# Routing and final residual of a slot-routing layer: one scaling moved to ScalarE, the last adds shared by two engines

## The chip, the cores and the metric

The kernel runs on one Trainium2 chip, on all 8 of its cores, each with its own batch element and its own copy of the weights. The cores do not talk to each other. The metric is the device time in microseconds (us) of the slowest core; the median over runs is given. Each core has TensorE (matmuls, output in PSUM), VectorE, ScalarE, GpSimd (here the adds that work on SBUF) and SyncE, which here only issues DMAs.

## The reference

Per batch element, `x` is 4096 tokens by 1024 channels in float32.

```python
x = x + _layernorm(_L0_attn_ref(_layernorm(x)))     # causal mean over the tokens
x = x + _layernorm(_L0_ffn_ref(_layernorm(x), ...)) # the part below
# inside _L0_ffn_ref, NUM_SLOTS = 64, TOP_K = 8
h = gelu(ctx @ w1 + b1)                             # ctx = [x, mean slot]
route_logits = (h @ w2 + b2) / (abs(tau) + 0.1)
alpha = softmax over the top 8 of 64 slots, zero elsewhere
slot_input = einsum('bts,btd->bsd', alpha, x)       # gathered into slots
# a GRU step, attention among the slots, a layernorm, a projection
slot_values = y @ wvp + bvp
out = einsum('bts,bsd->btd', alpha, slot_values)    # back to the tokens
return out @ wo + bo
```

## The kernel before

The 4096 tokens are 32 tiles of 128 (`NT = 32`), and the whole of `x` stays in SBUF as `sb_x` from the first load to the last store. The program is a row of stages, and in each every engine has its own instruction list; the order is written out by hand, with explicit semaphore waits. Helpers record the semaphore value after each ScalarE instruction (`SACT`, L207) and VectorE instruction (`VTS` L178, `VTT` L173, `VBN` L192 and so on), so that other engines can wait for it by name, as `V(("fn", j), 0)`.

1. First residual: layernorm of each tile (`x1b`), causal sums with triangular matmuls into two PSUM tiles (`pcs`), a second layernorm (`anb`, two halves), and GpSimd adds `anb` to `sb_x` (L412).
2. Router: layernorm (`x3b` on ScalarE), transpose, matmuls with `w1`, gelu, matmul with `w2`; the logits end up in `sb_L`.
3. Routing, L600 to L651, for each tile `j`: VectorE finds the 8 largest logits (`VMX`, MAX8) and a bias (`eb`), ScalarE takes the exp (`sb_E`), VectorE masks and sums it (`aub`), takes the reciprocal and writes `sb_alpha`, and then scales the tile of `sb_x` by the layernorm's scale to bf16 in `x2bf`, two halves in turn. TensorE multiplies `sb_alpha` with `x2bf` into `p_si` and transposes `sb_alpha` into `p_at`, and every fourth tile VectorE copies four transposed tiles to `sb_alphaT`, for which it waits for TensorE.
4. Slots: SyncE loads `Wih` transposed into `whhT` once TensorE has finished all routing tiles; then the GRU step, the attention and the projections follow, on 64 slots, fed by weights that are loaded piece by piece. Its last result is `sb_sv2`.
5. Final residual, L1057 to L1125. For each tile TensorE multiplies `sb_alphaT` with `sb_sv2` into `p_f` (L1074), two PSUM tiles in turn. VectorE works on pairs of tiles: four BATCH_NORM_STATS2 instructions, then eight small ones (`combine`) for mean and variance. ScalarE makes 1/sqrt from them by Ln and Exp (`rs5`), VectorE makes scale and bias (`p5`), ScalarE writes the normalised tile to the one buffer `fnb`, and GpSimd adds `fnb` to `sb_x` (L1115). ScalarE waits for that add before it writes `fnb` again (L1105 and L1106), and TensorE waits for `fnb` of tile `j - 2` before it refills a PSUM tile. SyncE stores four tiles at a time (L1122) and at the end waits for all stores.

In stages 3 and 5 the lines of the program order, the semaphores `sP3T` (TensorE's routing tiles) and `sX5` (GpSimd's adds) are what the change touches.

Of the kernel before, what the change touches and what calls it, by code (L numbers as in the profile page):

```python
# [7 lines left out]
F32 = mybir.dt.float32  # L8
BF16 = mybir.dt.bfloat16
AF = mybir.ActivationFunctionType  # L10
OP = mybir.AluOpType
# [14 lines left out]
P = 128  # L26
NT = 32
D = 1024
DH = 512
# [50 lines left out]
def _build(stage, prev=None):  # L80
    V = (prev or {}).get
    _DBG3 = globals()['_DBG3']
    nc = bass.Bass("TRN2", target_bir_lowering=False)
# [33 lines left out]
    with es:  # L117
        sbt = lambda name, shp, dt=F32: es.enter_context(nc.sbuf_tensor(name, shp, dt))
        sem = lambda name: es.enter_context(nc.semaphore(name))
# [52 lines left out]
        def VTT(out, a, b_, op):  # L172
            return gv.emit([out], [a, b_], lambda: v_.tensor_tensor(out, a, b_, op=op))  # L173

        def VTS(out, a, s1, s2, op0, op1=None):
            ins = [a] + [x for x in (s1, s2) if x is not None and not isinstance(x, float)]
            if op1 is None:
                return gv.emit([out], ins, lambda: v_.tensor_scalar(out, a, s1, None, op0=op0))  # L178
            return gv.emit([out], ins, lambda: v_.tensor_scalar(out, a, s1, s2, op0=op0, op1=op1))
# [11 lines left out]
        def VBN(out, a):  # L191
            return gv.emit([out], [a], lambda: v_.bn_stats(out, a))  # L192
# [17 lines left out]
        def SC(k, j, n=1):  # L210
            return stat[:, k * NT + j:k * NT + j + n]
# [388 lines left out]
        @blk.vector  # L600
        def _(v):
            for j in range(NT):
                v.wait_ge(sSSG, V(("lg", j // 8), 0))
                lt = sb_L[:, j * NS:(j + 1) * NS]
                val["m8", j] = VMX(m8b[:], lt)
                val["eb", j] = VTT(zcol[:, 1:2], m8b[:, 0:1], sb_ninv[:], OP.mult)
                v.wait_ge(sSSG, V(("exp", j), 0))
                ev_ = sb_E[:, (j % 2) * NS:(j % 2 + 1) * NS]
                au = aub[:, (j % 2) * NS:(j % 2 + 1) * NS]
                val["au", j] = VSTT(au, lt, m8b[:, 7:8], ev_, OP.is_ge, OP.mult, accum=zcol[:, 0:1])  # L610
                VRC(zcol[:, 2:3], zcol[:, 0:1])
                if j >= 2:
                    v.wait_ge(sP3T, j - 1)
                val["alf", j] = VTS(sb_alpha[:, j * NS:(j + 1) * NS], au, zcol[:, 2:3], None, OP.mult)
                val["x2b", j] = VTS(x2bf[:, (j % 2) * D:(j % 2 + 1) * D], sb_x[:, j * D:(j + 1) * D],
                                    SC(SM_S3, j), None, OP.mult)
                if j % 4 == 3:
                    v.wait_ge(sP3T, j + 1)
                    val["ate", j // 4] = VCP(sb_alphaT[:, (j - 3) * P:(j + 1) * P], p_at[0:NS, :])

        @blk.scalar
        def _(sc):
            sc.preload_act_table(AF.Exp)
            for j in range(NT):
                sc.wait_ge(sSVG, V(("eb", j), 0))
                if j >= 2:
                    sc.wait_ge(sSVG, V(("au", j - 2), 0))
                val["exp", j] = SACT(sb_E[:, (j % 2) * NS:(j % 2 + 1) * NS],
                                     sb_L[:, j * NS:(j + 1) * NS], AF.Exp,
                                     bias=zcol[:, 1:2], scale=sb_invt[:])  # L630

        @blk.tensor
        def _(t):
            t.wait_ge(sSVG, V("ghe", 0))
            t.wait_ge(sSSG, V(("lg", 3), 0))
            t.wait_ge(sSVG, V(("xte", NT - 1), 0))
            t.wait_ge(sSSG, V(("gel", NT - 1), 0))
            for j in range(NT):
                t.wait_ge(sSVG, V(("alf", j), 0))
                t.wait_ge(sSVG, V(("x2b", j), 0))  # L640
                alv = sb_alpha[:, j * NS:(j + 1) * NS]
                x2v = x2bf[:, (j % 2) * D:(j % 2 + 1) * D]
                for h in range(2):
                    t.matmul(p_si[0:NS, h * DH:(h + 1) * DH], alv, x2v[:, h * DH:(h + 1) * DH],  # L644
                             start=(j == 0), stop=(j == NT - 1))
                t.matmul(p_d2[0:NS, 0:1], alv, b3bf[:, j:j + 1],
                         start=(j == 0), stop=(j == NT - 1))
                if j % 4 == 0 and j >= 4:
                    t.wait_ge(sSVG, V(("ate", j // 4 - 1), 0))
                ins = t.transpose(p_at[0:NS, (j % 4) * P:(j % 4 + 1) * P], alv, c_eye[:])  # L650
                ins.then_inc(sP3T, 1)  # L651


        if stage >= 3:
# [34 lines left out]
            sGIc = sem("sGIc")  # L689
            sWSc = sem("sWSc")  # L690
            sX5 = sem("sX5")

            @blk.gpsimd
            def _(g):
# [347 lines left out]
            if _DBG3:  # L1042
                @blk.gpsimd
                def _(g):
# [9 lines left out]
                    g.dma_start(out=dbg3[:, 7 * D:7 * D + 24 * NS // 2], in_=sb_gh[:, 0:768]).then_inc(sDBG, 16)  # L1054
                    g.wait_ge(sDBG, 128)
            es4s2.close()
            fnb = sb4("fnb", [P, D])  # L1057
            es4pD.close()
            es4pA.close()
            es5p = ExitStack()  # L1060
            p_f = [es5p.enter_context(nc.psum_tensor("p_f0", [P, D], F32)),
                   es5p.enter_context(nc.psum_tensor("p_f1", [P, D], F32))]

            @blk.tensor
            def _(t):
                t.wait_ge(sSSG, V("sv2e", 0))
                t.wait_ge(sSVG, V(("ate", NT // 4 - 1), 0))
                for j in range(NT):
                    if j >= 2:
                        t.wait_ge(sSSG, V(("fn", j - 2), 0))  # L1070
                        t.wait_ge(sSVG, V(("bn5", (j - 2) // 2), 0))
                    pf = p_f[j % 2]
                    for h in range(2):
                        ins = t.matmul(pf[:, h * DH:(h + 1) * DH],  # L1074
                                       sb_alphaT[:, j * P:(j + 1) * P],
                                       sb_sv2[:, h * DH:(h + 1) * DH],
                                       start=True, stop=True)
                    ins.then_inc(sCS, 1)

            @blk.vector  # L1080
            def _(v):
                for pr in range(NPAIR):
                    v.wait_ge(sCS, NT + 2 * pr + 2)
                    for j in (2 * pr, 2 * pr + 1):
                        VBN(bn6x[:, j * 12:j * 12 + 6], p_f[j % 2][:, 0:DH])
                        val["bn5", pr] = VBN(bn6x[:, j * 12 + 6:j * 12 + 12], p_f[j % 2][:, DH:D])
                    val["c5", pr] = combine(SM_MX, SM_VX, bn6x, 2 * pr, 2, None)
                    v.wait_ge(sSSG, V(("rs5", pr), 0))
                    VTS(tmp4[:, 48:48 + 2], SC(SM_MX, 2 * pr, 2), -0.25, None, OP.mult)
                    val["p5", pr] = VTT(SC(SM_B1, 2 * pr, 2), tmp4[:, 48:48 + 2], SC(SM_S1, 2 * pr, 2), OP.mult)  # L1090

            @blk.scalar
            def _(sc):
                if _DBG3:
                    sc.wait_ge(sDBG, 128)
                for j in range(NT + 2):
                    if j % 2 == 0 and j >= 2 and (j - 2) // 2 < NPAIR:
                        pr = (j - 2) // 2
                        sc.wait_ge(sSVG, V(("c5", pr), 0))
                        SACT(SC(SM_G1, 2 * pr, 2), SC(SM_VX, 2 * pr, 2), AF.Ln)  # L1100
                        val["rs5", pr] = SACT(SC(SM_S1, 2 * pr, 2), SC(SM_G1, 2 * pr, 2), AF.Exp, scale=-0.5)
                    if j >= 2 and (j - 2) < NT:
                        jj = j - 2
                        sc.wait_ge(sSVG, V(("p5", jj // 2), 0))
                        if jj >= 1:  # L1105
                            sc.wait_ge(sX5, jj)  # L1106
                        val["fn", jj] = SACT(fnb[:],
                                             p_f[jj % 2][:], AF.Identity,
                                             bias=SC(SM_B1, jj), scale=SC(SM_S1, jj))

            @blk.gpsimd
            def _(g):
                for j in range(NT):
                    g.wait_ge(sSSG, V(("fn", j), 0))
                    g.tensor_tensor(sb_x[:, j * D:(j + 1) * D], fnb[:],  # L1115
                                    sb_x[:, j * D:(j + 1) * D], op=OP.add).then_inc(sX5, 1)

            @blk.sync
            def _(s):
                for gg in range(8):  # L1120
                    s.wait_ge(sX5, 4 * gg + 4)
                    s.dma_start(out=out_r[:, 4 * gg:4 * gg + 4, :],  # L1122
                                in_=sb_x[:].rearrange("p (j c) -> p j c", c=D)[:, 4 * gg:4 * gg + 4, :]
                                ).then_inc(sOUT, 16)
                s.wait_ge(sOUT, 8 * 16)  # L1125
# [61 lines left out]
```

## Time and profile before

| | |
|---|---|
| median of 2 runs | 1066.88 us (1064.89 to 1068.87) |
| the profiled execution | 1066.56 us, span 1065.0 us on its slowest core, core 7 |
| spans of the 8 cores | 1038.1 to 1065.0 us |
| busy, share of the span | TensorE 40%, VectorE 30%, ScalarE 21%, GpSimd 15% |
| stages of core 7, rounded | first residual to 340 us, statistics for the router to 400, router to 605, routing to 710, slots to 869, final residual to the end |

The span runs from the first to the last instruction of one core. Busy shares are means over stages that have different limits, so a change in one stage is read from that stage. Start times are microseconds from the beginning of the span, all of core 7. A timeline row gives the start, the duration, the engine and line, the operation and its operands as output<-inputs, and in brackets how long the engine had been idle and what released it. The line is often that of a helper, so the tile's name tells which instruction it is.

### The profile page before, as it was taken

How to read it: one execution, taken by the hardware profiler on the slowest of the kernel's cores; microseconds unless marked ns; L12 is line 12 of the kernel's file. 1: busy time of each engine (PE TensorE's matmuls, PEld its weight loads, DVE VectorE, ACT ScalarE, POOL GpSimd, SP SyncE). 2: the span in 40 equal slices, each digit the busy share in tenths (PEclk: the TensorE clock that was granted, in tenths of full speed). 3: DMA queues.
4: the chain of work that ended last, by engine and by line, in shares of the span. 5: the costliest groups of instructions: out<-in, count | busy, mean ns of one | idle time of the engine just before them, and what ended most of it. 6: DMA issues, size and time to landing. Idle time of an engine off the chain costs nothing.

```text
span 1065.0 us, 8876 instructions; the slowest of 8 cores (1038.1 to 1065.0 us)
## 1 busy us (share of the span) xinstructions
PE 426.3 (40%) x2610; PEld 196.5 (18%) x2610; DVE 320.9 (30%) x1080; ACT 226.1 (21%) x298; POOL 165.0 (15%) x91
## 2 busy tenths in 40 slices
PE   0032553435442028878887633331214741111110
PEld 0000000000000016656666411111201100000000
DVE  0034325353356861010111255560011012332331
ACT  0013333323323012222233211110010002222221
POOL 2002331313313000000000100000000004434433
PEclk9985555555555555585589755555555555555555
DMA  8979899996001000020113000015412222211122
GB/s 205 274 242 138 99 119 98 119 110 69 0 0 30 0 1 18 14 52 10 30 31 60 2 0 1 0 30 112 101 54 80 79 59 79 79 79 79 79 117 120
DMA packets 69294, 76.40 MB, mean 72 GB/s; under 512 B 53216, under 2 KB 57312, under 8 KB 68640
## 3 DMA queue, kind: packets, MB, share of 16 engines
q0 software_dynamic: 4800, 22.25, 18.5%
q1 hardware_dynamic: 64448, 53.60, 17.2%
q8 instruction: 22, 0.36, 0.1%
q14 instruction: 24, 0.20, 0.1%
HBM read 68.72 MB, written 36.70 MB: 99 GB/s over the span
## 4 chain that ended last, share of the span: by engine, by line
PE 31%; DVE 29%; ACT 11%; issue 10%; DMA 7%; another core or an unknown queue 6%; POOL 4%; DVEq 1%; ACTq 1%; POOLq 0%; SPq 0%
DVE bn6x L192 11%; PE p_h L541 10%; DVE bn6c L192 4%; ACT fnb L207 4%; DMA whhT<-wih_bf 4%; POOL sb_x L1115 4%; PE pcs L386 3%; PE pcs L394 3%; PE p_h L545 2%; DVE x2bf L178 2%; ACT anb L207 2%; PE p_xt L531 2%; PE p_f L1074 2%; PE ptot L398 1%
## 5 line engine op out<-in xcount | busy, mean ns | idle before, releaser
L541 PE MATMUL p_h<-x3t,sb_w1a 128*128 128x128 bf16 x1024 | 110.7, 273 | 37.7 <-DVE x3t L195 24.6
L412 POOL TENSOR_TENSOR sb_x<-anb,sb_x 128x1024 f32<-128x1024 f32 x32 | 75.4, 2377 | 181.0 <-ACT anb L207 181.0
L1115 POOL TENSOR_TENSOR sb_x<-fnb,sb_x 128x1024 f32<-128x1024 f32 x32 | 74.8, 2337 | 134.2 <-ACT fnb L207 134.2
L541 PEld LDWEIGHTS p_h<-x3t,sb_w1a 128*128 128x128 bf16 x1024 | 82.3, 122 | 53.1 <-issue 43.9
L1074 PE MATMUL p_f<-sb_sv,sb_alphaT 64*128 64x512 bf16 x64 | 32.1, 606 | 145.0 <-ACT fnb L207 143.6
L386 PE MATMUL pcs<-x1b,s_tri 128*128 128x512 bf16 x64 | 32.7, 615 | 142.1 <-ACT anb L207 137.8
L192 DVE BATCH_NORM_STATS2 bn6c<-pcs 128x6 f32<-128x512 f32 x64 | 39.9, 686 | 134.8 <-PE pcs L394 129.4
L195 DVE COPY x3t<-p_xt 128x1024 bf16<-128x1024 bf16 x32 | 22.1, 692 | 185.7 <-PE p_xt L531 185.7
L207 ACT ACTIVATE stat<-stat 128x2 f32<-128x2 f32 (+1 forms) x64 | 13.1, 204 | 305.0 <-DVE stat L184 303.5
L192 DVE BATCH_NORM_STATS2 bn6x<-sb_x 128x6 f32<-128x512 f32 x128 | 77.5, 679 | 0.0
L192 DVE BATCH_NORM_STATS2 bn6x<-p_f 128x6 f32<-128x512 f32 x64 | 39.9, 686 | 118.2 <-PE p_f L1074 118.2
L644 PE MATMUL p_si<-x2bf,sb_alpha 128*64 128x512 bf16 x64 | 33.0, 619 | 65.7 <-DVE m8b L201 52.8
L207 ACT ACTIVATE htb<-p_h 128x512 bf16<-128x512 f32 x32 | 19.1, 597 | 156.4 <-PE p_h L545 151.8
L531 PE MATMUL p_xt<-s_eye,x3b 128*128 128x128 bf16 x256 | 26.8, 268 | 62.6 <-ACT x3b L207 62.6
L207 ACT ACTIVATE fnb<-p_f,stat 128x1024 f32<-128x1024 f32 x32 | 38.5, 1204 | 53.9 <-POOL sb_x L1115 42.1
L696 POOL DMA_DIRECT2D sb_bz<-bih x1 | 0.5, 522 | 266.9 <-PE p_gh L574 266.9
L207 ACT ACTIVATE x1b<-sb_x,stat 128x1024 bf16<-128x1024 f32 x32 | 39.2, 1229 | 7.0 <-DVE stat L173 7.0
L207 ACT ACTIVATE x3b<-sb_x,stat 128x1024 bf16<-128x1024 f32 x32 | 39.3, 1231 | 0.0
L207 ACT ACTIVATE anb<-pcs,stat 128x1024 f32<-128x1024 f32 x32 | 37.8, 1185 | 0.0
L1074 PEld LDWEIGHTS p_f<-sb_sv,sb_alphaT 64*128 64x128 bf16 x64 | 4.4, 102 | 172.7 <-issue 172.7
L386 PEld LDWEIGHTS pcs<-x1b,s_tri 128*128 128x128 bf16 x64 | 4.3, 108 | 169.4 <-issue 169.4
L545 PE MATMUL p_h<-s_one,sb_c 1*128 1x128 bf16 x128 | 33.1, 259 | 0.0
(173 smaller groups left out, 542.5 us busy)
## 6 DMA issues: line engine op xcount, KB each, us to landing
sb_x<-x SPq DMA_DIRECT2D x8, 2048.0 KB, 39.1
out<-sb_x SPq DMA_DIRECT2D x8, 2048.0 KB, 6.7
whh_bf<-Whh POOLq DMA_DIRECT2D x1, 6144.0 KB, 56.4
wih_bf<-Wih POOLq DMA_DIRECT2D x1, 6144.0 KB, 113.7
wv_bf<-wv POOLq DMA_DIRECT2D x1, 2048.0 KB, 141.4
wvp_bf<-wvp POOLq DMA_DIRECT2D x1, 2048.0 KB, 159.7
wo_bf<-wo POOLq DMA_DIRECT2D x1, 2048.0 KB, 178.2
wst<-wv_bf SPq DMA_DIRECT2D x8, 256.0 KB, 2.6
```

The source lines that it names most:

```text
L192: return gv.emit([out], [a], lambda: v_.bn_stats(out, a))
L195: return gv.emit([out], [a], lambda: v_.tensor_copy(out, a))
L207: lambda: s_.activation(out, in_, func, bias=bias, scale=scale, accum_out=accum))
L386: ins = t.matmul(b[:, h * DH:(h + 1) * DH], c_tri[:], x1t[:, h * DH:(h + 1) * DH], start=True, stop=(j == 0))
L394: ins = t.matmul(b[:, h * DH:(h + 1) * DH], c_tri[0:1, :], carry[:, h * DH:(h + 1) * DH], start=False, stop=True)
L412: g.tensor_tensor(sb_x[:, j * D:(j + 1) * D], anb[:, (j % 2) * D:(j % 2 + 1) * D], sb_x[:, j * D:(j + 1) * D], op=OP.add).then_inc(sX2, 1)
L531: ins = t.transpose(p_xt[:, dc * P:(dc + 1) * P], x3v[:, dc * P:(dc + 1) * P], c_eye[:])
L541: t.matmul(ph[:, jc * P:(jc + 1) * P], w1av[:, dc, jc * P:(jc + 1) * P], x3tv[:, dc * P:(dc + 1) * P], start=(jc == 0 and dc == 0), stop=F ...
L545: ins = t.matmul(ph[:, jc * P:(jc + 1) * P], sb_c[:, jc * P:(jc + 1) * P], c_one[0:1, :], start=False, stop=(jc == 3))
L644: t.matmul(p_si[0:NS, h * DH:(h + 1) * DH], alv, x2v[:, h * DH:(h + 1) * DH], start=(j == 0), stop=(j == NT - 1))
L1074: ins = t.matmul(pf[:, h * DH:(h + 1) * DH], sb_alphaT[:, j * P:(j + 1) * P], sb_sv2[:, h * DH:(h + 1) * DH], start=True, stop=True)
L1115: g.tensor_tensor(sb_x[:, j * D:(j + 1) * D], fnb[:], sb_x[:, j * D:(j + 1) * D], op=OP.add).then_inc(sX5, 1)
```

## The change

- Stage 3: the scaling of `sb_x` into `x2bf` leaves VectorE's list and is an Identity activation with a scale on ScalarE, behind the exp of the same tile. Its wait for TensorE (the buffer's earlier use) goes with it, and TensorE now waits for ScalarE's semaphore.
- Stage 5: `p_f` has four PSUM tiles instead of two, and `fnb` two halves. GpSimd adds only the even tiles; the odd ones are added on VectorE, at the top of the next pair's work, and count a new semaphore `sX5o`. ScalarE waits for the add of tile `jj - 2` instead of `jj - 1`. SyncE's stores wait for both semaphores.

```diff
@@ routing, VectorE
                 val["alf", j] = VTS(sb_alpha[:, j * NS:(j + 1) * NS], au, zcol[:, 2:3], None, OP.mult)
-                val["x2b", j] = VTS(x2bf[:, (j % 2) * D:(j % 2 + 1) * D], sb_x[:, j * D:(j + 1) * D],
-                                    SC(SM_S3, j), None, OP.mult)
@@ routing, ScalarE, behind the exp
+                if j >= 2:
+                    sc.wait_ge(sP3T, j - 1)
+                val["x2b", j] = SACT(x2bf[:, (j % 2) * D:(j % 2 + 1) * D],
+                                     sb_x[:, j * D:(j + 1) * D], AF.Identity,
+                                     scale=SC(SM_S3, j))
@@ routing, TensorE
-                t.wait_ge(sSVG, V(("x2b", j), 0))
+                t.wait_ge(sSSG, V(("x2b", j), 0))
@@ final residual, buffers
-            fnb = sb4("fnb", [P, D])
+            fnb = sb4("fnb", [P, 2 * D])
-            p_f = [es5p.enter_context(nc.psum_tensor("p_f0", [P, D], F32)),
-                   es5p.enter_context(nc.psum_tensor("p_f1", [P, D], F32))]
+            p_f = [es5p.enter_context(nc.psum_tensor(f"p_f{i}", [P, D], F32))
+                   for i in range(4)]
@@ final residual, TensorE
-                    if j >= 2:
-                        t.wait_ge(sSSG, V(("fn", j - 2), 0))
-                        t.wait_ge(sSVG, V(("bn5", (j - 2) // 2), 0))
-                    pf = p_f[j % 2]
+                    if j >= 4:
+                        t.wait_ge(sSSG, V(("fn", j - 4), 0))
+                        t.wait_ge(sSVG, V(("bn5", (j - 4) // 2), 0))
+                    pf = p_f[j % 4]
@@ final residual, VectorE
                 for pr in range(NPAIR):
+                    if pr >= 1:
+                        jo = 2 * pr - 1
+                        v.wait_ge(sSSG, V(("fn", jo), 0))
+                        v.tensor_tensor(sb_x[:, jo * D:(jo + 1) * D], fnb[:, (jo % 2) * D:(jo % 2 + 1) * D],
+                                        sb_x[:, jo * D:(jo + 1) * D], op=OP.add).then_inc(sX5o, 1)
                     v.wait_ge(sCS, NT + 2 * pr + 2)
...
+                jo = NT - 1
+                v.wait_ge(sSSG, V(("fn", jo), 0))
+                v.tensor_tensor(sb_x[:, jo * D:(jo + 1) * D], fnb[:, (jo % 2) * D:(jo % 2 + 1) * D],
+                                sb_x[:, jo * D:(jo + 1) * D], op=OP.add).then_inc(sX5o, 1)
@@ final residual, ScalarE
-                        if jj >= 1:
-                            sc.wait_ge(sX5, jj)
-                        val["fn", jj] = SACT(fnb[:],
-                                             p_f[jj % 2][:], AF.Identity,
+                        if jj >= 2:
+                            sc.wait_ge(sX5 if jj % 2 == 0 else sX5o, jj // 2)
+                        val["fn", jj] = SACT(fnb[:, (jj % 2) * D:(jj % 2 + 1) * D],
+                                             p_f[jj % 4][:], AF.Identity,
@@ final residual, GpSimd
-                for j in range(NT):
+                for j in range(0, NT, 2):
@@ final residual, SyncE
-                    s.wait_ge(sX5, 4 * gg + 4)
+                    s.wait_ge(sX5, 2 * gg + 2)
+                    s.wait_ge(sX5o, 2 * gg + 2)
```

## Rows read from the trace of the kernel before

**Rows 1.** Busy times in two stages: window, PE, PEld, DVE, ACT, POOL, clock, DMA share, GB/s:
```profile
605.00:710.00 105.00, 38.89 (x147) 17.64 (x143) 58.50 (x233) 17.22 (x35) 4.62 (x6) 0.51 0.02 1
...
869.00:1065.00 196.00, 32.10 (x64) 4.43 (x64) 60.41 (x224) 45.31 (x65) 74.78 (x32) 0.50 0.22 86
```

**Rows 2.** Waits in 860 to 1066: waiter <- releaser, us, times, longest:
```profile
ACT fnb L207 <- POOL sb_x L1115: 42.1, 16, 2.6
```

**Rows 3.** Timeline of one pair in the final residual:
```profile
952.94 2.49 DVE L192 BATCH_NORM_STATS2 bn6x<-p_f 128x6 f32<-128x512 f32 x4 [6.61 <-PE p_f L1074]
...
956.82 0.50 ACT L207 ACTIVATE stat<-stat 128x2 f32<-128x2 f32 x2 [5.24 <-DVE stat L184]
...
957.70 0.16 DVE L173 TENSOR_TENSOR stat<-tmp,stat 128x2 f32<-128x2 f32 x1
958.06 1.20 ACT L207 ACTIVATE fnb<-p_f,stat 128x1024 f32<-128x1024 f32 x1 [0.74 <-DVE stat L173]
959.41 2.34 POOL L1115 TENSOR_TENSOR sb_x<-fnb,sb_x 128x1024 f32<-128x1024 f32 x1 [5.35 <-ACT fnb L207]
...
961.89 1.20 ACT L207 ACTIVATE fnb<-p_f,stat 128x1024 f32<-128x1024 f32 x1 [2.63 <-POOL sb_x L1115]
...
963.35 1.01 PE L1074 MATMUL p_f<-sb_sv,sb_alphaT 64*128 64x512 bf16 x2 [2.83 <-ACT fnb L207]
964.46 2.49 DVE L192 BATCH_NORM_STATS2 bn6x<-p_f 128x6 f32<-128x512 f32 x4 [6.61 <-PE p_f L1074]
```

**Rows 4.** Timeline: statistics of the first and last pair, and the last add:
```profile
871.45 2.49 DVE L192 BATCH_NORM_STATS2 bn6x<-p_f 128x6 f32<-128x512 f32 x4 [18.91 <-PE p_f L1074]
...
1045.33 2.49 DVE L192 BATCH_NORM_STATS2 bn6x<-p_f 128x6 f32<-128x512 f32 x4 [6.61 <-PE p_f L1074]
...
1055.63 2.34 POOL L1115 TENSOR_TENSOR sb_x<-fnb,sb_x 128x1024 f32<-128x1024 f32 x1 [1.50 <-ACT fnb L207]
```

**Rows 5.** Timeline of the routing stage: one tile, a fourth tile, the next copy:
```profile
612.64 0.22 DVE L201 MAX8 m8b<-sb_L 128x8 f32<-128x64 f32 x1
...
613.33 0.44 ACT L207 ACTIVATE sb_E<-sb_L,zcol,sb_invt 128x64 f32<-128x64 f32 x1 [2.30 <-DVE zcol L173]
...
614.71 0.75 DVE L178 TENSOR_SCALAR x2bf<-sb_x,stat 128x1024 bf16<-128x1024 f32 x1
615.37 0.22 DVE L201 MAX8 m8b<-sb_L 128x8 f32<-128x64 f32 x1
...
617.44 0.75 DVE L178 TENSOR_SCALAR x2bf<-sb_x,stat 128x1024 bf16<-128x1024 f32 x1
...
618.34 1.03 PE L644 MATMUL p_si<-x2bf,sb_alpha 128*64 128x512 bf16 x2 [1.54 <-DVE x2bf L178]
...
619.63 0.42 DVE L195 COPY sb_alphaT<-p_at 64x512 bf16<-64x512 bf16 x1 [1.44 <-PE p_at L650]
...
632.42 0.41 DVE L195 COPY sb_alphaT<-p_at 64x512 bf16<-64x512 bf16 x1 [1.44 <-PE p_at L650]
```

**Rows 6.** Groups by form: operation, shapes, xcount, busy us, mean ns, idle before:
```profile
L207 ACT ACTIVATE x3b<-sb_x,stat 128x1024 bf16<-128x1024 f32 x32 | 39.3, 1231 | 0.0
...
L490 ACT ACT_TABLE_LOAD x1 | 1.3, 1283 | 0.0
L623 ACT ACT_TABLE_LOAD x1 | 1.3, 1283 | 0.0
...
L173 DVE TENSOR_TENSOR tn<-tn 128x512 f32<-128x512 f32 x1 | 0.7, 692 | 0.1
```

**Rows 7.** SyncE's waits as issuer of DMAs:
```profile
SPq L710 <- PE p_at L650: 125.4, 1, 125.4
```

**Rows 8.** Timeline: a small VectorE add alone, and beside two GpSimd adds:
```profile
135.36 0.17 DVE L173 TENSOR_TENSOR tmp<-bn6x 128x16 f32<-128x16 f32 x1
...
334.37 4.72 POOL L412 TENSOR_TENSOR sb_x<-anb,sb_x 128x1024 f32<-128x1024 f32 x2 [7.46 <-ACT anb L207]
...
337.77 1.35 DVE L173 TENSOR_TENSOR tmp<-bn6x 128x16 f32<-128x16 f32 x1
```

More of the change, by code:

```diff
@@ L691, in _build @@
             sX5 = sem("sX5")
+            sX5o = sem("sX5o")
             @blk.gpsimd
@@ L1082, in _ @@
                 for pr in range(NPAIR):
+                    if pr >= 1:
[3 more added lines that the diff above has]
+                                        sb_x[:, jo * D:(jo + 1) * D], op=OP.add).then_inc(sX5o, 1)
                     v.wait_ge(sCS, NT + 2 * pr + 2)
                     for j in (2 * pr, 2 * pr + 1):
-                        VBN(bn6x[:, j * 12:j * 12 + 6], p_f[j % 2][:, 0:DH])
-                        val["bn5", pr] = VBN(bn6x[:, j * 12 + 6:j * 12 + 12], p_f[j % 2][:, DH:D])
+                        VBN(bn6x[:, j * 12:j * 12 + 6], p_f[j % 4][:, 0:DH])
+                        val["bn5", pr] = VBN(bn6x[:, j * 12 + 6:j * 12 + 12], p_f[j % 4][:, DH:D])
                     val["c5", pr] = combine(SM_MX, SM_VX, bn6x, 2 * pr, 2, None)
@@ L1112, in _ @@
             def _(g):
-                for j in range(NT):
+                for j in range(0, NT, 2):
                     g.wait_ge(sSSG, V(("fn", j), 0))
-                    g.tensor_tensor(sb_x[:, j * D:(j + 1) * D], fnb[:],
+                    g.tensor_tensor(sb_x[:, j * D:(j + 1) * D], fnb[:, (j % 2) * D:(j % 2 + 1) * D],
                                     sb_x[:, j * D:(j + 1) * D], op=OP.add).then_inc(sX5, 1)
```

## The prediction

> **What bounds the kernel now.** I read the busy times by stage first. In the last stage, where the second residual is added, 196 us pass while no engine is busy for more than 75 us of them; in the routing stage VectorE is busy 58.5 of 105 us, far more than any other engine [rows 1]. Neither stage is limited by an engine's throughput, so I went to the waits and then to the order of instructions. In the last stage ScalarE sat idle 42.1 us in 16 waits for GpSimd's add [rows 2]: one wait per pair of tiles, 2.6 us each.
>
> The timeline of one pair shows why. From the start of the statistics (952.94) to the last small VectorE instruction that makes scale and bias (957.70 + 0.16) are 4.92 us. Then `fnb` of the even tile starts 0.20 later and takes 1.20, GpSimd's add starts 0.15 after it and takes 2.34, and only then does `fnb` of the odd tile start (961.89), because there is one `fnb` buffer. TensorE refills that odd PSUM tile at 963.35, and the next statistics start at 964.46 [rows 3]. It is one closed ring of 11.52 us; nothing overlaps. Over the stage the first statistics start at 871.45 and those of the sixteenth pair at 1045.33, which makes 173.88 / 15 = 11.59 us per pair; after the last pair's scale and bias (1045.33 + 4.92 = 1050.25) it takes until 1055.63 + 2.34 = 1057.97, 7.72 us, before the last add ends [rows 4].
>
> In the routing stage the reader is to see VectorE's chain. A tile starts with MAX8 at 612.64, the exp starts at 613.33, `x2bf` follows `sb_alpha` at 614.71, and the next MAX8 starts only at 615.37: 2.73 us per tile. The fourth tile of a group is longer, for VectorE then waits for the transposes: `x2bf` at 617.44 ends 618.19, TensorE starts at 618.34, and the copy to `sb_alphaT` starts at 619.63, the next such copy at 632.42. So a group of four takes 12.79 us, and there are eight [rows 5].
>
> **The change part by part.**
>
> *`x2bf` from VectorE to ScalarE.* It takes 0.75 us on VectorE [rows 5]; on ScalarE the nearest row is `x3b`, the same scaled read of `sb_x` to bf16, at 1.231 us [rows 6]. VectorE: without it the next MAX8 takes its place at 614.71 instead of 615.37, which saves 0.66 and makes the tile 2.07 us. Does ScalarE cover its 1.23? The exp starts at 613.33 and takes 0.44 (`sb_E`, [rows 5]), so `x2bf` occupies ScalarE until 615.00. The next exp is wanted 0.69 after its MAX8, at 614.71 + 0.69 = 615.40. It fits with 0.4 us to spare, so I cost it at nothing; with the cover gone each microsecond of lateness would be paid 32 times. Queued behind the moved instruction is the next exp, and its new wait, that TensorE has finished tile j - 2, is long met: TensorE's tile takes some 1.2 us of 2.07. In the fourth tile what TensorE waits for moves less. The exp starts 1.38 before the old `x2bf` (613.33 to 614.71), so at 616.06; plus 0.44 plus 1.23 gives 617.73 against 618.19: 0.46 saved. A group saves 3 x 0.66 + 0.46 = 2.44 us. ScalarE instructions that follow directly may overlap by 0.1 us, so I take 2.5, and eight groups give **20.0 us**. Bounds: 16 (the fourth tile gains nothing: 8 x 1.98) to 21 (it gains 0.66 like the others: 8 x 2.64). The DMA queue's next work, the transposing loads of `whhT`, waits for exactly these tiles of TensorE (125.4 us in one wait, [rows 7]) and so moves forward with them; the saving is passed on.
>
> *Four PSUM tiles instead of two.* TensorE's 1.0 us and its wait leave the ring: the next pair's matmuls are done before VectorE asks. But in the new program order VectorE still waits for `fnb` of the odd tile, adds it, and only then starts the next pair's statistics. So the ring stays closed through VectorE; the statistics of the next pair stand behind the added wait. By themselves four tiles save about 1.2 us a pair.
>
> *Two `fnb` halves, odd tiles added on VectorE.* The odd `fnb` no longer waits for GpSimd; it follows the even one directly. VectorE's f32 add of 128x1024 is not in the trace. 128x512 takes 692 ns [rows 6] and 128x16 takes 0.17 [rows 8]: (0.692 - 0.17) / 496 = 1.05 ns an element, so 1.23 us for 1024. Left alone it would start 0.20 + 1.20 + 1.20 + 0.15 = 2.75 after scale and bias, while GpSimd's add of the even tile runs from 1.55 to 3.89. Here one row decides. At the end of the first residual stage two GpSimd adds run without a break from 334.37 to 339.09, and a VectorE add of 128x16 with both inputs in SBUF, normally 0.17 us, takes 1.35: it starts at 337.77 and ends at 339.12, 0.03 after GpSimd's add [rows 8].  So a two-input VectorE add stands still until the running GpSimd add is over. The Trainium skill ("SBUF — State Buffer", Who interferes with whom) says that a VectorE instruction with two SBUF inputs and a GpSimd instruction that reads SBUF shut each other out for a whole instruction; by that rule, the trace agrees.
>
> I therefore let VectorE's add end 1.09 after GpSimd's: 1.23 less the 0.14 that the small one had done of its 0.17 when the way came free. The new ring: 4.92 + 0.20 + 1.20 + 0.15 + 2.34 + 1.09 - 0.06 (the next statistics start slightly before the add ends, as MAX8 at 615.37 starts before `x2bf` ends at 615.46 in [rows 5]) = 9.84 us against 11.52. It saves 1.68 x 15 = **25.2 us**. The tail is 0.20 + 1.20 + 0.15 + 2.34 + 1.09 = 4.98 against 7.72: **2.7 us**. Bounds for the blocked add: 1.05 to 1.25 after GpSimd's, 2 us in all either way. The output DMAs wait for both adds; a pair's data now comes every 9.84 us, and the queues were busy 22% of the stage [rows 1], so they stay hidden.
>
> Sum: 20.0 + 25.2 + 2.7 = 47.9 us. The profiled execution took 1066.56 us (its span 1065.0 and 1.6 around it), so 1018.7; the median of the runs is 1066.88, 0.3 above, and I leave the forecast at **1018.7 us**.
>
> **The rivals.**
>
> *B: the two adds overlap freely.* For it: the one stretched row is a small instruction at the end of a stage, and no long VectorE add is shown beside GpSimd. Against it: that row ends within 0.03 of GpSimd's end, which is hard to get by chance. The ring would be 4.92 + 2.75 + 1.23 - 0.06 = 8.84 us, saving 40.2, the tail 3.98, saving 3.7; with the 20.0 the time is 1066.6 - 63.9 = 1002.7 us.
>
> *C: a table load at every switch between exp and Identity (ends slower than before).* One ACT_TABLE_LOAD takes 1283 ns; the exp loop has one ahead of it, at L623, the gelu loop one at L490 [rows 6]. If Identity were not in the loaded table, ScalarE would need 0.44 + 1.28 + 1.23 + 1.28 = 4.23 us per tile, 135.4 us for 32, against 8 x 12.79 = 102.3: 33.1 slower, and with 27.9 saved in the last stage 1071.8 us. It decides as soon as ScalarE's tile is longer than 2.07 us (break-even of the whole change at 4.07). Against it: in the gelu stage 32 Identity instructions (`x3b`) alternate with gelu behind a single load [rows 6]. The Trainium skill ("ScalarE: Activation LUTs", Table sets: the hidden batching unit) puts identity in every set; by that rule this case is out, and no run here has shown it for exp.
>
> *D: the routing stage's gain is given back* in what follows, as the `whhT` loads or the weights are late. The kernel would take 1038.7 us. Against it: the queue's longest wait there is for TensorE, not for data [rows 7].
>
> *E: TensorE's clock.* It is granted 0.50 to 0.51 in both changed stages, the 1.2 GHz level [rows 1]. Closer work could lift it to 2.4 GHz; only the fourth tile's 1.2 us would gain, under 5 us in all, or nothing. Conversely the rest of the kernel keeps its clock; the cores' spans differ today by 27 us (table of the profile, above) for reasons the change doesn't touch, and this spread is the largest uncertainty of the likeliest case.
>
> **How the numbers follow.** The likeliest (blocked add) has 0.80, with its own range 1012 to 1025 (bounds of the terms, plus a few us of clock). B has 0.10, D 0.04, C 0.03, E in full 0.03. To leave out no more than 2 in 10, 1006 to 1026 suffices: the lower end goes halfway to B. About 2% is what a measurement can tell from no change, 21 us: the likeliest, B, E and D are all faster by more (D by 28), C is within 2%. I keep 0.01 for something slower. Faster 0.95, same 0.04, slower 0.01.
>
> **What would show each step.** In the changed kernel: MAX8 to MAX8 2.07 us and copy to copy of `sb_alphaT` about 10.3; `x2bf` on ScalarE 1.23 with no load between; pairs 9.84 apart; VectorE's add lasting about 2.3 us in the records, ending 1.1 after GpSimd's (B: 1.23 us long); the last add ending 5.0 after the last scale and bias. Wrong would be made the sum by ScalarE starting its exp late, by GpSimd's add growing beyond 2.34 beside VectorE, or by a change in the middle of the kernel that the diff doesn't touch.

## The result and the profile after

The changed kernel takes 1015.19 us (median of 11 runs, 1007.93 to 1028.74) against 1068.9 us for the kernel before (10 runs, 1059.24 to 1089.92). The ratio is 0.953, 95% interval 0.947 to 0.959, which is 44 to 57 us of 1068.9. The forecast was 1018.7 us, 47.9 us less than the profiled execution of before. Some executions of every kernel run longer than the rest, so medians here are taken over all runs and ratios over the undisturbed ones alone, and the two need not divide out.

The profiled execution of the changed kernel took 1022.9 us, span 1021.1 us on core 3. The spans of its eight cores lie between 981.2 and 1021.1 us, so single times are compared with care, and the experiments below are read from the lengths of the changed stages, which a shift of everything before them does not touch. The mean distance of a pair's statistics shows how steady these lengths are: it is 11.58 or 11.59 us on all eight cores before and 9.83 or 9.84 after.

First the routing stage, in the kernel before: the copies to `sb_alphaT` and the exps (duration in ns as min/median/max, then the first and the last start).

```profile
L195 DVE COPY sb_alphaT<-p_at x8: 415/417/418, 619.6 to 709.7; 64x512 bf16<-64x512 bf16 x8
L207 ACT ACTIVATE sb_E<-sb_L,zcol,sb_invt x32: 439/439/440, 607.8 to 706.1; 128x64 f32<-128x64 f32 x32
```

The same two, and `x2bf`, in the kernel after.

```profile
L195 DVE COPY sb_alphaT<-p_at x8: 416/417/417, 625.2 to 697.9; 64x512 bf16<-64x512 bf16 x8
...
L207 ACT ACTIVATE sb_E<-sb_L,zcol,sb_invt x32: 439/439/441, 615.9 to 694.7; 128x64 f32<-128x64 f32 x32
...
L207 ACT ACTIVATE x2bf<-sb_x,stat x32: 1132/1132/1134, 616.2 to 695.1; 128x1024 bf16<-128x1024 f32 x32
```

From the first exp to the last copy it was 709.7 - 607.8 = 101.9 us, and it is 697.9 - 615.9 = 82.0 us: 19.9 us less. The timeline of one group answers to [rows 5]:

```profile
627.59 0.22 DVE L201 MAX8 m8b<-sb_L 128x8 f32<-128x64 f32 x1
...
628.28 0.44 ACT L207 ACTIVATE sb_E<-sb_L,zcol,sb_invt 128x64 f32<-128x64 f32 x1 [0.59 <-DVE zcol L173]
628.62 1.13 ACT L207 ACTIVATE x2bf<-sb_x,stat 128x1024 bf16<-128x1024 f32 x1
...
629.66 0.22 DVE L201 MAX8 m8b<-sb_L 128x8 f32<-128x64 f32 x1
...
634.41 1.03 PE L647 MATMUL p_si<-x2bf,sb_alpha 128*64 128x512 bf16 x2 [1.15 <-ACT x2bf L207]
...
635.71 0.42 DVE L195 COPY sb_alphaT<-p_at 64x512 bf16<-64x512 bf16 x1 [1.55 <-PE p_at L653]
```

MAX8 to MAX8 is 2.07 us; within a group of four ScalarE is idle 0.59 us before most exps (0.87 or 0.88 before three), which is the cover left over; no table load stands between exp and `x2bf`. In the fourth tile TensorE is now released by ScalarE's `x2bf`.

Now one pair of the final residual in the changed kernel, which answers to [rows 3]:

```profile
905.71 2.48 DVE L192 BATCH_NORM_STATS2 bn6x<-p_f 128x6 f32<-128x512 f32 x4
...
910.45 0.16 DVE L173 TENSOR_TENSOR stat<-tmp,stat 128x2 f32<-128x2 f32 x1
910.82 2.30 ACT L207 ACTIVATE fnb<-p_f,stat 128x1024 f32<-128x1024 f32 x2 [0.75 <-DVE stat L173]
912.17 2.34 POOL L1128 TENSOR_TENSOR sb_x<-fnb,sb_x 128x1024 f32<-128x1024 f32 x1 [7.46 <-ACT fnb L207]
912.27 2.10 PE L1078 MATMUL p_f<-sb_sv,sb_alphaT 64*128 64x512 bf16 x4 [7.61 <-ACT fnb L207]
913.22 2.37 DVE L1090 TENSOR_TENSOR sb_x<-fnb,sb_x 128x1024 f32<-128x1024 f32 x1 [2.61 <-ACT fnb L207]
915.51 0.69 DVE L192 BATCH_NORM_STATS2 bn6x<-p_f 128x6 f32<-128x512 f32 x1
```

The pair takes 915.51 - 905.71 = 9.80 us instead of 11.52. VectorE's add starts at 913.22 while GpSimd's runs to 912.17 + 2.34 = 914.51, and it ends at 915.59, 1.08 later. It is idle 2.61 us before its add. The first and the last statistics, and the last adds, answer to [rows 4]:

```profile
856.74 2.49 DVE L192 BATCH_NORM_STATS2 bn6x<-p_f 128x6 f32<-128x512 f32 x4 [18.87 <-PE p_f L1078]
...
1004.26 2.48 DVE L192 BATCH_NORM_STATS2 bn6x<-p_f 128x6 f32<-128x512 f32 x4
...
1010.71 2.34 POOL L1128 TENSOR_TENSOR sb_x<-fnb,sb_x 128x1024 f32<-128x1024 f32 x1 [7.46 <-ACT fnb L207]
1011.77 2.37 DVE L1102 TENSOR_TENSOR sb_x<-fnb,sb_x 128x1024 f32<-128x1024 f32 x1 [2.61 <-ACT fnb L207]
```

(1004.26 - 856.74) / 15 = 9.83 us a pair against 11.59: 173.9 - 147.5 = 26.4 us less. The last add ends at 1014.14, which is 9.88 us after the last statistics started; before it was 1057.97 - 1045.33 = 12.64: 2.8 us less. Together 19.9 + 26.4 + 2.8 = 49.1 us are found in the changed stages of two profiled cores, inside the 44 to 57 of the runs. The two profiled executions themselves differ by only 43.6 us (1066.56 and 1022.92), because the stages ahead of the routing, which the change does not touch, ended 8.1 us later in the one after (first exp at 615.9 against 607.8). Between the stages, from the last copy to the first statistics, before took 871.45 - 709.7 = 161.8 us and after 856.74 - 697.9 = 158.8; in the ten experiments, which change nothing there, it was 155.4 to 162.8. Those 3 us are scatter, not gain.

### The profile page after: what moved, and what is told of

Its sections match the earlier page's. It is cut to its first block, busy times and chain, and to the rows that moved or that the text cites. A ratio compares the mean times of both kernels' runs of the same rounds, so it can differ in the third digit from the quotient of the medians.

```text
span 1021.1 us, 8923 instructions; the slowest of 8 cores (981.2 to 1021.1 us)
## 1 busy us (share of the span) xinstructions
PE 425.9 (42%) x2610; PEld 199.8 (20%) x2610; DVE 336.4 (33%) x1064; ACT 257.5 (25%) x330; POOL 127.5 (12%) x75
## 3 DMA queue, kind: packets, MB, share of 16 engines
q0 software_dynamic: 4800, 22.25, 19.4%
## 4 chain that ended last, share of the span: by engine, by line
PE 31%; DVE 28%; issue 14%; ACT 10%; DMA 7%; another core or an unknown queue 7%; DVEq 1%; ACTq 1%; SPq 0%
DVE bn6x L192 12%; PE p_h L541 10%; DVE bn6c L192 4%; DMA whhT<-wih_bf 4%; PE pcs L386 3%; PE pcs L394 3%; PE p_h L545 2%; PE p_xt L531 2%; ACT fnb L207 2%; ACT anb L207 2%; DVE x3t L195 2%; PE ptot L398 1%; PE pcs L390 1%; ACT x3b L207 1%
## 5 line engine op out<-in xcount | busy, mean ns | idle before, releaser
L541 PE MATMUL p_h<-x3t,sb_w1a 128*128 128x128 bf16 x1024 | 113.2, 278 | 37.8 <-DVE x3t L195 27.0
L1078 PE MATMUL p_f<-sb_sv,sb_alphaT 64*128 64x512 bf16 x64 | 31.8, 607 | 108.1 <-ACT fnb L207 105.5
L1128 POOL TENSOR_TENSOR sb_x<-fnb,sb_x 128x1024 f32<-128x1024 f32 x16 | 37.5, 2342 | 141.3 <-ACT fnb L207 141.3
L1090 DVE TENSOR_TENSOR sb_x<-fnb,sb_x 128x1024 f32<-128x1024 f32 x15 | 35.6, 2370 | 39.1 <-ACT fnb L207 39.1
L207 ACT ACTIVATE x2bf<-sb_x,stat 128x1024 bf16<-128x1024 f32 x32 | 36.2, 1132 | 0.0
```

What stands on the lines that cost most here:

```text
L207: lambda: s_.activation(out, in_, func, bias=bias, scale=scale, accum_out=accum))
L541: t.matmul(ph[:, jc * P:(jc + 1) * P], w1av[:, dc, jc * P:(jc + 1) * P], x3tv[:, dc * P:(dc + 1) * P], start=(jc == 0 and dc == 0), stop=F ...
L1078: ins = t.matmul(pf[:, h * DH:(h + 1) * DH], sb_alphaT[:, j * P:(j + 1) * P], sb_sv2[:, h * DH:(h + 1) * DH], start=True, stop=True)
L1090: v.tensor_tensor(sb_x[:, jo * D:(jo + 1) * D], fnb[:, (jo % 2) * D:(jo % 2 + 1) * D], sb_x[:, jo * D:(jo + 1) * D], op=OP.add).then_inc(s ...
L1128: g.tensor_tensor(sb_x[:, j * D:(j + 1) * D], fnb[:, (j % 2) * D:(j % 2 + 1) * D], sb_x[:, j * D:(j + 1) * D], op=OP.add).then_inc(sX5, 1)
```

## The experiments

The theory has three parts: (1) the routing gain comes from taking `x2bf` out of VectorE's chain, under cover of ScalarE's spare time; (2) in the final residual VectorE's add stands still behind a running GpSimd add; (3) the ring stays closed through VectorE's wait for the odd `fnb`. The rivals are a gain that is given back, an add that is simply slow, and a ring that closes elsewhere. "A pair" is always the mean distance of the statistics over 15 intervals. The diffs are against the changed kernel where nothing else is said, and ... stands for lines left out.

| kernel | four routing tiles, us | pair, us | kernel, us (runs) |
|---|---|---|---|
| before | 12.87 | 11.59 | 1064.75 to 1070.99 |
| changed | 10.39 | 9.83 | 1015.19 (11) |
| routing half alone | 10.40 | 11.57 | 1043.86 (1) |
| final half alone | 12.86 | 9.86 | 1036.89 (1) |
| four PSUM tiles, GpSimd adds all, one `fnb` | 10.40 | 7.80 | 989.11 (4) |
| parities swapped | 10.40 | 7.60 | 985.79 (4) |
| all adds on VectorE, ahead of statistics | 10.39 | 8.76 | 1002.35 (3) |
| GpSimd adds all, VectorE never waits | 10.40 | 7.77 | 987.18 (4) |
| all adds on VectorE, moved back | 10.39 | 6.13 | 963.9 (6) |
| `x2bf` twice on ScalarE | 12.99 | 9.85 | 1041.33 (1) |
| `x2bf` on VectorE in its wait, adds as in 963.9 | 10.34 | 6.15 | 962.29 (4) |
| GpSimd's adds beside the statistics | 10.40 | 5.26 | 954.3 (8) |

The first column of numbers is the distance of the first and the last copy to `sb_alphaT`, divided by 7. For before, the last column gives the range of the medians beside which the experiments ran. On the eight cores of one kernel the pair agrees within 0.02 us, but for one core at 6.05 beside seven at 6.13.

### The halves by themselves

The routing half alone keeps the final residual of before (two of its lines):

```diff
-            fnb = sb4("fnb", [P, 2 * D])
+            fnb = sb4("fnb", [P, D])
...
-                for j in range(0, NT, 2):
+                for j in range(NT):
```

> The routing half of the change alone (x2bf on ScalarE; final residual as before). Theory: in the routing stage the copies to sb_alphaT stand about 10.3 us apart (12.79 before) and the stage is about 20 us shorter; the final residual keeps its 11.59 us a pair; the kernel takes about 1048 us. Rival (the gain of the routing stage is given back while whhT is loaded): the copies stand closer, but the final residual does not start earlier against the start of the routing stage.

The final half alone puts `x2bf` back on VectorE, behind `sb_alpha`:

```diff
+                val["x2b", j] = VTS(x2bf[:, (j % 2) * D:(j % 2 + 1) * D], sb_x[:, j * D:(j + 1) * D],
+                                    SC(SM_S3, j), None, OP.mult)
...
-                val["x2b", j] = SACT(x2bf[:, (j % 2) * D:(j % 2 + 1) * D],
-                                     sb_x[:, j * D:(j + 1) * D], AF.Identity,
...
```

> The final-residual half alone (x2bf stays on VectorE). Theory: the routing stage keeps 12.79 us for four tiles, a pair of the final residual takes 9.83 us as in the changed kernel, and the last add ends 5.0 us after the last scale and bias; about 1039 us. If the two halves helped each other, the pair would not be at 9.83.

Each half moves only its own stage: 10.40 and 11.57, 12.86 and 9.86. Beside 1064.75 us of before they save 21 and 28 us, one run each; together 49. With the routing half alone the first statistics come 849.16 - 688.7 = 160.5 us after the last copy (161.8 before), so the routing gain is passed on whole and rival D is out.

### Where VectorE's add starts

The parities are swapped: VectorE adds the even tiles, GpSimd the odd ones.

```diff
-                        jo = 2 * pr - 1
+                        jo = 2 * pr - 2
...
-                            sc.wait_ge(sX5 if jj % 2 == 0 else sX5o, jj // 2)
+                            sc.wait_ge(sX5o if jj % 2 == 0 else sX5, jj // 2)
...
-                for j in range(0, NT, 2):
+                for j in range(1, NT, 2):
```

> The changed kernel with the parities swapped: VectorE adds the even tiles, GpSimd the odd ones. VectorE's add then starts before GpSimd's. Theory (a two-input VectorE instruction stands still only behind a running GpSimd add): VectorE's add takes 1.23 us instead of 2.37, a pair takes 4.92 + 0.20 + 1.20 + 0.15 + 1.23 - 0.06 = 7.6 us instead of 9.83, the kernel about 33 us less than the changed one, some 982 us. Rival (the f32 add on VectorE simply takes 2.37 us): the add stays at 2.37 and a pair takes 8.8 us, 1000 us.

The two adds of a pair in that kernel's timeline, and the statistics behind them:

```profile
903.90 2.30 ACT L207 ACTIVATE fnb<-p_f,stat 128x1024 f32<-128x1024 f32 x2 [0.74 <-DVE stat L173]
905.21 1.22 DVE L1090 TENSOR_TENSOR sb_x<-fnb,sb_x 128x1024 f32<-128x1024 f32 x1 [1.51 <-ACT fnb L207]
...
906.34 2.34 POOL L1128 TENSOR_TENSOR sb_x<-fnb,sb_x 128x1024 f32<-128x1024 f32 x1 [5.40 <-ACT fnb L207]
906.35 2.48 DVE L192 BATCH_NORM_STATS2 bn6x<-p_f 128x6 f32<-128x512 f32 x4
```

The same instruction on the same shapes takes 1.22 us here and 2.37 us in the changed kernel. It is not slow; it waited. A pair takes 7.60 us, which shortens the stage by 15 x 2.23 = 33 us against the changed kernel, and the kernel takes 985.79 us, 29 us less by the medians: all from a swap of which engine takes which tile. The statistics beside GpSimd's add keep their 2.48 us.

### Without GpSimd

All adds go to VectorE, both of a pair ahead of the next pair's statistics. The helper `VADD` waits for `fnb` of the tile and adds it.

```diff
                     if pr >= 1:
-                        jo = 2 * pr - 1
-                        v.wait_ge(sSSG, V(("fn", jo), 0))
-                        v.tensor_tensor(...)
+                        VADD(v, 2 * pr - 2)
+                        VADD(v, 2 * pr - 1)
...
```

> The changed kernel with all 32 adds on VectorE, both of a pair ahead of the next pair's statistics; GpSimd adds nothing. Theory: each add takes 1.23 us, since nothing runs beside it; a pair takes 4.92 + 1.55 + 1.23 + 1.23 - 0.15 = 8.8 us against 9.83, so VectorE alone is faster than VectorE and GpSimd together; about 998 us. Rival (VectorE's add takes 2.37 us in itself): a pair takes 11.1 us, slower than the changed kernel by 19 us.

The adds take 1.22 us (median of 32), a pair 8.76 us, the kernel 1002.35 us. VectorE does twice the adds and is faster than with GpSimd's help as the change arranged it.

### The four PSUM tiles alone

Beside the routing half, only the PSUM tiles and the distances of their waits are changed; there is one `fnb` and GpSimd adds every tile. The diff is against the kernel before.

```diff
-            p_f = [es5p.enter_context(nc.psum_tensor("p_f0", [P, D], F32)),
-                   es5p.enter_context(nc.psum_tensor("p_f1", [P, D], F32))]
+            p_f = [es5p.enter_context(nc.psum_tensor(f"p_f{i}", [P, D], F32))
+                   for i in range(4)]
...
-                    if j >= 2:
-                        t.wait_ge(sSSG, V(("fn", j - 2), 0))
+                    if j >= 4:
+                        t.wait_ge(sSSG, V(("fn", j - 4), 0))
...
```

> With the new routing stage, the final residual of before with four PSUM tiles and nothing else: one fnb, all 32 adds on GpSimd, no add on VectorE. The prediction said that four tiles alone save 1.2 us of 11.6 a pair, to about 10.4; the kernel would then take about 1025 us. Rival, which reads the new order of the wait as the cost: VectorE starts the next statistics at once, and the ring is fnb, GpSimd add, fnb: 2 x (1.20 + 0.15 + 2.34 + 0.14) = 7.7 us a pair, with the small two-input VectorE instructions hidden or held up behind the adds; about 15 x 1.9 = 29 us less than the changed kernel, 3 us back at the end: about 989 us.

A pair takes 7.80 us on the mean, and the kernel 989.11 us: the four tiles alone save 11.59 - 7.80 = 3.79 us a pair, three times what the prediction gave them, and twice what the whole change saves. The time of 1025 us that followed from the prediction's 1.2 us did not come; the 989 us of the rival written down beside it did. One pair of that kernel:

```profile
902.77 2.49 DVE L192 BATCH_NORM_STATS2 bn6x<-p_f 128x6 f32<-128x512 f32 x4
903.03 1.20 ACT L207 ACTIVATE fnb<-p_f,stat 128x1024 f32<-128x1024 f32 x1 [2.59 <-DVE stat L173]
904.38 2.34 POOL L1118 TENSOR_TENSOR sb_x<-fnb,sb_x 128x1024 f32<-128x1024 f32 x1 [1.84 <-ACT fnb L207]
905.36 0.16 DVE L188 TENSOR_REDUCE stat<-bn6x 128x2 f32<-128x8 f32 x1
905.44 1.30 DVE L173 TENSOR_TENSOR tmp<-bn6x 128x8 f32<-128x8 f32 x1
...
908.21 2.34 POOL L1118 TENSOR_TENSOR sb_x<-fnb,sb_x 128x1024 f32<-128x1024 f32 x1 [1.50 <-ACT stat L207]
...
908.56 2.01 DVE L178 TENSOR_SCALAR tmp<-stat 128x2 f32<-128x2 f32 x1 [0.88 <-ACT stat L207]
```

The statistics start at 902.77, 0.26 us before the first `fnb` of the pair ahead: without the add in its list VectorE goes on at once. What bounds this kernel is `fnb` and GpSimd in turn, and one small instruction on VectorE stands still behind each of the two adds: the one at 905.44 ends at 906.74 (GpSimd's add at 906.72), the one at 908.56 at 910.57 (910.55).

The next kernel gives GpSimd's adds two `fnb` halves as well, and still no add to VectorE.

```diff
-                    if pr >= 1:
-                        jo = 2 * pr - 1
-                        v.wait_ge(sSSG, V(("fn", jo), 0))
-                        v.tensor_tensor(...)
...
-                            sc.wait_ge(sX5 if jj % 2 == 0 else sX5o, jj // 2)
+                            sc.wait_ge(sX5, jj - 1)
...
-                for j in range(0, NT, 2):
+                for j in range(NT):
```

> Four PSUM tiles and two fnb halves, but all adds on GpSimd and no add on VectorE, so that VectorE never waits for fnb. By busy times alone a pair would take 4.9 us (VectorE's statistics to scale and bias; GpSimd needs 4.7): about 942 us. Theory of the exclusion: the small VectorE instructions with two SBUF inputs between the statistics and scale and bias each stand still behind a GpSimd add, first to the end of the one, then to the end of the other; a pair takes about 8 us and the kernel about 989 us, with TENSOR_TENSOR rows of 128x8 or 128x2 lasting one to two us instead of 0.16.

A pair takes 7.77 us, not 4.9. VectorE's groups by form in the final residual of that kernel:

```profile
L173 DVE TENSOR_TENSOR tmp<-stat 128x2 f32<-128x2 f32 x16 | 31.8, 1984 | 0.0
L173 DVE TENSOR_TENSOR tmp<-bn6x 128x8 f32<-128x8 f32 x16 | 19.4, 1210 | 0.0
...
L173 DVE TENSOR_TENSOR stat<-tmp,stat 128x2 f32<-128x2 f32 x16 | 2.6, 162 | 1.7
```

Two instructions of two and eight elements a row take 31.8 + 19.4 = 51.2 us of the stage, where at 0.16 us each they would take 5: 46 us, or 2.9 us a pair, is what parts 7.77 from 4.9. The second `fnb` half brought nothing here (7.80 and 7.77).

### Off the ring

All adds on VectorE, but behind the work that they were in front of. The diff is against the kernel with the adds ahead of the statistics; only its added lines are shown.

```diff
+                    if pr >= 1:
+                        VADD(v, 2 * pr - 2)
                     val["c5", pr] = combine(SM_MX, SM_VX, bn6x, 2 * pr, 2, None)
+                    if pr >= 1:
+                        VADD(v, 2 * pr - 1)
                     v.wait_ge(sSSG, V(("rs5", pr), 0))
```

> All adds on VectorE, but moved off the ring: the even tile's add of the pair before stands behind this pair's statistics, the odd one's behind the eight small instructions, where VectorE else waits for ScalarE. Theory: VectorE never waits for fnb and is the bound: 2.49 + 1.23 + 1.29 + 1.23 + 0.44 = 6.7 us a pair against 9.83; about 48 us less than the changed kernel, some 966 us, the fastest of all. Rival (the ring through fnb or through TensorE's refill binds instead): a pair stays above 8 us.

VectorE's long instructions of one pair:

```profile
866.31 2.49 DVE L192 BATCH_NORM_STATS2 bn6x<-p_f 128x6 f32<-128x512 f32 x4
...
868.72 1.20 DVE L1086 TENSOR_TENSOR sb_x<-fnb,sb_x 128x1024 f32<-128x1024 f32 x1
...
870.96 1.23 DVE L1086 TENSOR_TENSOR sb_x<-fnb,sb_x 128x1024 f32<-128x1024 f32 x1
...
872.47 2.49 DVE L192 BATCH_NORM_STATS2 bn6x<-p_f 128x6 f32<-128x512 f32 x4
```

Neither add has an idle time of VectorE before it. A pair takes 6.13 us (the 6.7 expected left out that neighbours overlap by up to 0.1: the first add starts at 868.72, the statistics end at 868.80), the kernel 963.9 us, ratio to before 0.903 (0.896 to 0.911). Against the kernel with the same adds ahead of the statistics, the place alone is worth 2.63 us a pair. That is part (3).

The last step gives GpSimd the odd tiles again, but releases each add by the scale and bias of the next pair, so that it runs beside the statistics; `fnb` has four buffers, and the last two pairs stay on VectorE.

```diff
-            fnb = sb4("fnb", [P, 2 * D])
+            fnb = sb4("fnb", [P, 4 * D])
...
+                for q in range(NPAIR - 2):
+                    j = 2 * q + 1
+                    g.wait_ge(sSSG, V(("fn", j), 0))
+                    g.wait_ge(sSVG, V(("p5", q + 1), 0))
+                    g.tensor_tensor(sb_x[:, j * D:(j + 1) * D], fnb[:, (j % 4) * D:(j % 4 + 1) * D],
+                                    sb_x[:, j * D:(j + 1) * D], op=OP.add).then_inc(sX5o, 1)
```

> As e7_all_vector_late, but GpSimd adds the odd tiles of all but the last two pairs, each released by the scale and bias of the pair after it, so that its 2.34 us lie beside the four statistics instructions of VectorE (2.49 us, one input, from PSUM) and beside no two-input instruction; fnb has four buffers. Theory of the exclusion: the statistics are not disturbed, VectorE loses one add of 1.13 from its 6.13 us ring, and a pair takes about 5.0 us; about 17 us less than e7_all_vector_late, some 948 us. Rival (any GpSimd add costs VectorE what it saves): a pair takes 6 us or more.

```profile
887.15 2.49 DVE L192 BATCH_NORM_STATS2 bn6x<-p_f 128x6 f32<-128x512 f32 x4
887.35 2.34 POOL L1132 TENSOR_TENSOR sb_x<-fnb,sb_x 128x1024 f32<-128x1024 f32 x1 [3.25 <-DVE stat L173]
...
889.82 0.16 DVE L173 TENSOR_TENSOR tmp<-bn6x 128x8 f32<-128x8 f32 x1
...
890.87 1.23 DVE L1086 TENSOR_TENSOR sb_x<-fnb,sb_x 128x1024 f32<-128x1024 f32 x1
```

GpSimd's add ends at 889.69, 0.13 us before the first two-input instruction starts, and nothing is stretched. VectorE's one add a pair stands behind the small instructions. A pair takes 5.26 us; 5.0 was expected, which took 1.13 off the 6.13. The add that left had lasted 1.20 and overlapped both its neighbours by 0.08, and now the first small instruction starts 0.10 behind the statistics (889.74 against 889.64), so that only 0.94 comes off; the last 0.07 is not explained. The kernel takes 954.3 us over 8 runs (943.35 to 963.92), ratio to before 0.904 (0.893 to 0.914). The stage is shorter by 15 x 0.87 = 13 us than in the kernel of 963.9 us; whether the whole kernel is faster than that one stays open, since the two were not run side by side and their ratios are equal within the intervals. Both beat the changed kernel clearly.

### The routing stage

`x2bf` is computed twice on ScalarE:

```diff
+                for _rep in range(2):
-                val["x2b", j] = SACT(x2bf[:, (j % 2) * D:(j % 2 + 1) * D],
+                    val["x2b", j] = SACT(x2bf[:, (j % 2) * D:(j % 2 + 1) * D],
...
```

> The changed kernel with the scaling into x2bf done twice on ScalarE (the same values, written twice), to price the cover that the prediction costed at nothing. Theory: ScalarE had 0.4 to 0.6 us to spare per tile and now needs 1.03 more, so three tiles of four take about 2.5 to 2.6 us instead of 2.07, and the fourth 1.0 more; four tiles take about 12.8 us, as before the change, and the gain of the routing stage is gone, about 1033 us in all. Rival (ScalarE had much more room, or VectorE's chain does not pass through it): four tiles stay near 10.3.

Four tiles take 12.99 us against 12.87 before the change: the gain of the stage is gone.

```profile
639.33 2.37 ACT L207 ACTIVATE x2bf<-sb_x,stat 128x1024 bf16<-128x1024 f32 x2
641.61 0.42 ACT L207 ACTIVATE sb_E<-sb_L,zcol,sb_invt 128x64 f32<-128x64 f32 x1
641.94 2.37 ACT L207 ACTIVATE x2bf<-sb_x,stat 128x1024 bf16<-128x1024 f32 x2
```

Within a group ScalarE runs without a gap, 641.94 - 639.33 = 2.61 us a tile instead of 2.07: it has become the bound. The spare time that the prediction found (0.4 us) and the profile after shows (0.59 us) is all there was; what goes beyond it, 0.54 us a tile, is paid.

In the last kernel `x2bf` goes back to VectorE, between the bias and the wait for the exp, and the final residual is that of the 963.9 us kernel.

```diff
                 val["eb", j] = VTT(zcol[:, 1:2], m8b[:, 0:1], sb_ninv[:], OP.mult)
+                if j >= 2:
+                    v.wait_ge(sP3T, j - 1)
+                val["x2b", j] = VTS(x2bf[:, (j % 2) * D:(j % 2 + 1) * D], sb_x[:, j * D:(j + 1) * D],
+                                    SC(SM_S3, j), None, OP.mult)
                 v.wait_ge(sSSG, V(("exp", j), 0))
...
```

> As e7_all_vector_late, but x2bf back on VectorE, placed behind the bias (eb), where VectorE waits 0.75 us for the exp; ScalarE has only the exp. Theory: what cost time was x2bf's place in VectorE's chain, not its engine; a tile takes about 2.1 us and four about 10.4, as with ScalarE; the kernel ties with e7_all_vector_late within 3 us. Rival (the engine matters: x2bf delays the mask behind the exp): a tile takes 2.4 us or more, and the kernel is over 8 us slower than e7_all_vector_late.

Four tiles take 10.34 us and the kernel 962.29 us: a tie with 10.39 and 963.9. The stage gains as much if the instruction stays on VectorE and only moves into its wait; part (1) is about the place, not the engine.

## Why the prediction was right

- *The ring of 11.52 us and its length over the stage* stood; the final half alone and the routing half alone leave each other's numbers untouched.
- *`x2bf` to ScalarE:* 20.0 us forecast, 19.9 measured. ScalarE's instruction took 1.132 us, not the 1.231 of `x3b` [rows 6]. A tile is 2.07 us as forecast. Four tiles took 10.39 instead of 10.29: in some groups one exp or one MAX8 starts 0.28 us late (such an exp 0.65 instead of 0.37 after the bias's start); what delays it the profile does not show. The kernel before has the same delays, and its mean is 12.87, not the 12.79 of the one group in the rows, so the saving was hardly touched by them: 2.48 a group against 2.5.
- *The blocked add:* the deciding step, taken from the one row of 1.35 us [rows 8]. It was forecast to end 1.09 after GpSimd's and ended 1.08 after it, with a record 2.37 us long. The swapped parities show that the wait is the cause. The bounds given for it, 1.05 to 1.25, are 0.6 us less and 2.6 us more over 16 adds, not 2 us either way; nothing hung on that. Case B (free overlap, 1002.7 us) is out.
- *The new ring:* 9.84 forecast, 9.80 in the timeline, 9.83 on the mean; 25.2 us forecast, 26.4 measured, since the mean of before was 11.59 and not the 11.52 from which the sum took its 1.68.
- *The tail:* 2.7 forecast, 2.8 measured.
- *Case C (table loads):* out. Exp and Identity alternate 32 times behind a single load, at 614.57; the next one starts at 696.24, behind the last `x2bf`.
- *Case D (given back):* out, by the routing half alone.
- *The whole kernel:* that the median lies within 3.5 us of the forecast is in part luck, since the 11 runs spread over 21 us and the median of before moved from 1066.88 to 1068.9 with more runs. The terms above are what bears the forecast out.
- *Case E (the clock):* the granted clock stays at 0.50, the 1.2 GHz level, in both changed stages, as the two windows of core 3 show (window, then busy us and counts of PE, PEld, DVE, ACT and POOL, granted clock, DMA share, GB/s):

```profile
612.00:707.70 95.70, 41.64 (x187) 20.14 (x188) 44.05 (x207) 50.47 (x67) 4.32 (x6) 0.50 0.07 9
854.00:1021.00 167.00, 31.79 (x64) 4.74 (x64) 96.89 (x240) 43.86 (x65) 37.46 (x16) 0.50 0.26 101
```

One step was wrong, though the sum did not hang on it: "By themselves four tiles save about 1.2 us a pair". That took TensorE's matmuls and handoffs out of the old ring and kept the ring. In truth the ring broke at that point, because VectorE could start the next statistics while `fnb` and the adds went on, and the saving was 3.79 us. The prediction saw the wait that closed the ring again, but not that this made the added VectorE instruction a loss: without it and with one `fnb`, the ratio to before is 0.926 (0.921 to 0.931) instead of 0.953. The time forecast for the change as written was right; the reading that each part of it helps would have been wrong.

## What to carry to other kernels

A ring of waits is cut by the place of an instruction in its engine's list, so ask of every added instruction what stands behind its wait: here moving the same adds behind the next statistics was worth 2.63 us of 8.76. Before work is shared between VectorE and GpSimd, look whether the two would run at the same time with VectorE instructions that have two SBUF inputs, tiny ones too, or with a small SBUF-to-SBUF TENSOR_SCALAR; put GpSimd's work beside VectorE work that reads one input from PSUM. And measure each part of a change alone, since one part can hide that another costs.

## What the runs showed of the hardware

Not only VectorE instructions with two inputs stand still behind a GpSimd add. In the kernel with four PSUM tiles alone a TENSOR_SCALAR of 128x2 f32, one SBUF input, takes 1876 ns on the mean over 16:

```profile
L178 DVE TENSOR_SCALAR tmp<-stat 128x2 f32<-128x2 f32 x16 | 30.0, 1876 | 14.2 <-ACT stat L207 14.2
```

Its start and end fit the GpSimd add beside it as closely as for the two-input ones (above: 910.57 against 910.55). The Trainium skill ("SBUF — State Buffer", Who interferes with whom) says that a tensor_scalar which runs in a mode that uses both ports excludes GpSimd too; by that rule, the trace agrees. That the instruction ran in such a mode no record shows by itself. Not every VectorE instruction on SBUF is held: the TENSOR_REDUCE at 905.36, wholly beside GpSimd's add of 904.38 to 906.72, keeps its 0.16 us, and so do its like in the 15 pairs of that kernel where one runs beside an add. The statistics with an input in PSUM were not stretched in any kernel (678 to 686 ns on the mean, with and without GpSimd beside them). In the kernel that adds everything on GpSimd with two `fnb` halves, a VectorE instruction that stood behind the first of two adjoining GpSimd adds was let through between them, and the next one stood behind the second (1210 and 1984 ns on the mean).
